# Layer 1's feed-forward by expert tiles: rows scattered to 23 single-expert tiles, gathered weights, results gathered back

## The reference

```python
# layer 1, xn = layernorm(x), 2048 rows of 128
probs = softmax(xn @ gate_w.T)                  # 8 experts
top_idx, top_val = argmax(probs), max(probs)
top_val = top_val / (top_val + 1e-8)
onehot = one_hot(top_idx, 8)
xe = einsum('ne,nd->end', onehot, x_flat)       # a row is zero for all experts but its own
he = gelu(einsum('end,edh->enh', xe, expert_w1))    # 128 -> 256
ye = einsum('enh,ehd->end', he, expert_w2)          # 256 -> 128
out = einsum('end,ne->nd', ye, onehot) * top_val[:, None]
f = layernorm(out) * ln_gamma + ln_beta
# attention of layer 1: 16 heads of 8, window of 32 keys to either side
x = x + attn(xn) * silu(f)
```

## Time and profile before

| | |
|---|---|
| median of 3 runs | 1961.46 us (1961.2 to 1962.14) |
| span of the profiled execution | 1957.4 us |
| the profiled execution's own time | one of the three runs above, which of them is not told |
| median of the runs less the span | 4.1 us |
| TensorE, VectorE, ScalarE, POOL busy | 89%, 73%, 59%, 53% |
| mean granted TensorE clock | 0.951 |
| layer 1, first stage | 951.4 to 1095.6 us |
| layer 1, attention | 1095.6 to about 1312 us |

### The profile page before, as it was taken

The page is one execution under the profiler, slowest core; times in us unless marked ns, Lnnn a source line. Parts: engine busy times, 40 slices in busy tenths (PEclk is TensorE's granted clock), DMA queues, the critical chain, the costliest instruction groups (busy, mean ns, idle before and its releaser), DMA issues. The chain is left out here.

```text
span 1957.4 us, 34440 instructions
## 1 busy us (share of the span) xinstructions
PE 1744.6 (89%) x13171; PEld 1433.1 (73%) x13199; DVE 1421.3 (73%) x2911; ACT 1155.9 (59%) x2340; POOL 1040.4 (53%) x998
## 2 busy tenths in 40 slices
PE   6999999999999999899799788874798568999997
PEld 4888888888888888787567577763577445666676
DVE  6888888788888788534578677857767488777772
ACT  4677767676767777555367555552433344666665
POOL 4888999999999999920312134335257530110111
PEclk9999999999999999999889899986799878999999
DMA  3000000001000000000000000002045300000000
GB/s 90 14 1 15 1 15 1 15 1 36 1 1 1 1 1 1 28 1 1 20 11 22 1 2 2 2 23 69 23 109 133 78 12 1 2 2 2 2 2 23
DMA packets 52100, 37.44 MB, mean 19 GB/s; under 512 B 7560, under 2 KB 45864, under 8 KB 51936
## 3 DMA queue, kind: packets, MB, share of 16 engines
q1 hardware_dynamic: 45248, 30.53, 5.3%
q0 software_dynamic: 5632, 4.20, 1.5%
q10 hardware_dynamic: 1056, 0.52, 0.1%
HBM read 29.99 MB, written 5.24 MB: 18 GB/s over the span
## 5 line engine op out<-in xcount | busy, mean ns | idle before, releaser
L753 POOL TENSOR_TENSOR dtl<-dts,dth 128x512 fp32r<-128x512 f32 x256 | 356.5, 1392 | 20.5
L683 DVE TENSOR_REDUCE nm<-PS 128x1 f32<-128x1024 f32 x256 | 311.6, 1217 | 30.5 <-PE PS L203 29.6
L1930 ACT ACTIVATE ET_a<-PS 128x256 f32<-128x256 f32 (+2 forms) x512 | 223.0, 493 | 129.2 <-PE PS L1845 78.6
L751 POOL CAST dth<-dts 128x512 fp32r<-128x512 f32 x256 | 232.6, 909 | 48.6 <-ACT dts L610 47.5
L201 PE MATMUL PS<-xh,yh 128*128 128x512 f32 x512 | 225.5, 440 | 8.1 <-ACT G L603 4.0
L144 PE MATMUL PS<-C,XN 128*128 128x128 f32 x1120 | 176.3, 283 | 38.1 <-DVE XN L196 34.6
L203 PE MATMUL PS<-xh,yl 128*128 128x512 f32 x512 | 204.7, 400 | 0.0
L202 PE MATMUL PS<-xl,yh 128*128 128x512 f32 x512 | 204.4, 399 | 0.0
L1744 POOL TENSOR_SCALAR_AFFINE_SELECT ET_a<-ET_a 128x1024 f32<-128x1024 f32 x32 | 35.0, 1092 | 310.3 <-ACT ET_a L1930 310.3
L603 ACT ACTIVATE XNT<-PS,nm 128x1024 f32<-128x1024 f32 x128 | 142.8, 1115 | 68.5 <-DVE nm L683 67.3
L610 ACT ACTIVATE dts<-PS 128x512 f32<-128x512 f32 x256 | 152.7, 598 | 45.9 <-POOL dtl L753 43.1
(11 more groups left out here) (425 smaller groups left out, 4709.4 us busy)
## 6 DMA issues: line engine op xcount, KB each, us to landing
e_wg<-in_WgT SPq DMA_DIRECT2D x16, 256.0 KB, 2.8
e_wu<-in_WuT SPq DMA_DIRECT2D x16, 256.0 KB, 3.1
e_wd<-in_WdT SPq DMA_DIRECT2D x16, 256.0 KB, 4.0
X<-in_L_attn_X SPq DMA_DIRECT2D x2, 512.0 KB, 4.5
wqn<-in_L_attn_Wq SPq DMA_DIRECT2D x8, 128.0 KB, 2.1
wkn<-in_L_attn_Wk SPq DMA_DIRECT2D x8, 128.0 KB, 2.6
wvn<-in_L_attn_Wv SPq DMA_DIRECT2D x8, 128.0 KB, 2.4
won<-in_WoT SPq DMA_DIRECT2D x8, 128.0 KB, 2.6
```

The source lines that it names most:

```text
L683: e.tensor_reduce(self.nm[:, half, i:i + 1], self.S[half], AX.X, MAX, negate=True).then_inc(*self.top.up((g, half)))
L751: e.tensor_copy(hi, src).then_inc(*ts.up((g, g4, "h")))
L753: e.tensor_tensor(lo, src, f(hi), SUB).then_inc(*ts.up((g, g4, "l")))
L1930: e.activation(dst, src, ACT.Exp, scale=self.SC, bias=0.0).then_inc(*self.ex.up(it))
```

## The change

`Ffn1` is replaced by `Moe1`. Each row is computed for its own expert alone, in fp32 products without the three-way split.

In the first stage, after the one-hot choice, 18 small bf16 products count for each row how many rows ahead of it have its expert ("ranks"). VectorE makes of it, in 14 steps ("frac" to "row"), each row's place `pos` in a list in which each expert has whole tiles of 128 rows (23 tiles always suffice), and for each tile the row of its expert's weights. POOL zeroes a buffer of 23 tiles, which SP stores to DRAM as `m_x_rows`. The fence to the attention waits for "rk0", the value copies and POOL's last memset. The value copies go from VectorE to ScalarE.

In the attention stage POOL scatters the 16 blocks of rows (`XN`) to `m_x_rows`; SP waits for all 16 and loads the 23 tiles in six transfers; POOL gathers each tile's weights, 128 rows of 2 KB (both matrices), into a ring of 8 slots, a slot being free after the second product of the tile that held it. The jobs of the tiles, T (transpose four tiles), U (first product of two tiles, gelu) and D (second product, copy out), all stand at place (5, 0) of TensorE's and ScalarE's order, and the column products of head 0 wait for the last. SP stores the results, POOL gathers them back to `G` in row order behind the cuts 1 to 6, and multiplies by `top_val` behind the cuts 8 to 11. For this the row products use three banks in heads 0 to 4 and not six; `KH[2]` is cleared by ScalarE after heads 1 and 2; the layernorm steps of `Gate1` run two per head from head 18 on, with `rstd` before cut 17.

```diff
+    def scatter(self, e, q):
+        q.wait_ge(self.blank, "z")
+        q.wait_ge(self.route, "pos")
+        for n in range(NT):
+            e.indirect_dma_start(self.xd[:, :], bass.IndirectOffsetOnAxis(ap=self.pos[:, n:n + 1], axis=0), self.k.XN[:, n, :],
+                                 None).then_inc(*self.sorted.up(n))
+    def weights(self, e, q):
+        q.wait_ge(self.route, "row")
+        for j in range(self.TILES):
+            if j >= self.RING:
+                q.wait_ge(self.on_pe, ("D", (j - self.RING) // 2))
+            e.indirect_dma_start(self.W[:, j % self.RING, :], None, self.k.A["w12"],
+                                 bass.IndirectOffsetOnAxis(ap=self.row[:, j:j + 1], axis=0)).then_inc(*self.in_w[j % self.RING].up(j))
+    def back(self, e, q, x):
+        k = self.k
+        if 1 <= x <= 6:
+            if x == 1:
+                for g in range(6):
+                    q.wait_ge(self.stored[g], "y")
+            for n in range(3 * x - 3, min(3 * x, NT)):
+                e.indirect_dma_start(k.G[:, n, :], None, self.yd[:, :],
+                                     bass.IndirectOffsetOnAxis(ap=self.pos[:, n:n + 1], axis=0)).then_inc(*self.taken.up(n))
...
+        self.place = {}
+        for n_, x in enumerate(self.jobs):
+            self.place.setdefault((5, 0), []).append(x)
...
+    def lift(self, e, q, s):
+        o = self.k.bank(4 + s % 2)
+        q.wait_ge(self.on_act, ("T", s // 2))
+        if s >= 2:
+            q.wait_ge(self.on_act, ("U", s - 2))
+        for j in self.tiles(s):
+            q.wait_ge(self.in_w[j % self.RING], j)
+            for m in range(2):
+                c = 256 * (j % 2) + 128 * m
+                t = e.matmul(o[:, c:c + 128], self.W[:, j % self.RING, 128 * m:128 * m + 128],
+                             self.xT[s // 2 % 2][:, 128 * (j % 4):128 * (j % 4) + 128], start=True, stop=True)
+        t.then_inc(*self.on_pe.up(("U", s)))
...
-        rs, cs, rn, cn = list(range(6)), [], 0, 0
+        rs, cs, rn, cn = list(range(3 if kind == 1 else 6)), [], 0, 0
...
                 if self.kind == 1:
-                    q.wait_ge(self.clear_pool, "edge1")
+                    q.wait_ge(self.clear_edge, 1)
+                    q.wait_ge(self.moe.on_act, self.moe.on_act.last)
...
-            if self.gate and j == 3 and x >= 4 and late < len(self.gate.steps):
+            if self.gate and j in (3, 8) and x >= 18 and late < len(self.gate.steps):
                 self.gate.dve_step(e, q, late)
```

More of the change, by code:

```diff
@@ L1235, in pe, with act @@
                 n = 4 * c + j
-                t = e.matmul(k.bank(4 + c)[:, 128 * j:128 * j + 128], k.XNT[:, 128 * n:128 * n + 128], w.WV, start=True, stop=True)
+                t = e.matmul(k.bank(self.banks[c])[:, 128 * j:128 * j + 128], k.XNT[:, 128 * n:128 * n + 128], w.WV, start=True, stop=True)
             t.then_inc(*self.done.up(c))
+    def act(self, e, q):
+        k, w = self.k, self.w
+        for c in range(4):
+            q.wait_ge(self.done, c)
+            e.activation(w.va[:, 4 * c:4 * c + 4, :, 0:8], k.bank(self.banks[c]).rearrange("p (n h d) -> p n h d", n=4, h=16),
+                         ACT.Copy).then_inc(*self.ready.up(c))
     def dve(self, e, q):
@@ L1368, in pool @@
-    def pool(self, e, q):
[L1369 to L1375, removed]
+        q.wait_ge(self.on_pool, "xs0")
@@ L1432, in act @@
+        e.matmul(flat(self.rank[:, 0:NT, :]), self.bb[:, :], flat(self.oh[:, :, :]), start=True, stop=True)
+        for t0 in range(NT):
+            a = t0 + 1 if t0 else 1
+            n = (NT + 1 if t0 else NT) - a
+            src = bc(self.oh[:, t0, :], [128, 8, n]).rearrange("p e n -> p n e")
+            t = e.matmul(self.rank[:, a:a + n, :], self.ob[:, :], src, start=False, stop=True, skip_group_check=True)
+        t.then_inc(*self.route_pe.up("ranks"))
     def act(self, e, q):
-        k = self.k
@@ new lines, in drop @@
+    def drop(self, e, q, s):
+        q.wait_ge(self.on_act, ("U", s))
+        if s >= 2 and s % 2 == 0:
+            q.wait_ge(self.on_act, ("D", s - 1))
+        for j in self.tiles(s):
+            o = self.k.bank(6)[:, 128 * (j % 4):128 * (j % 4) + 128]
+            for m in range(2):
+                c = 256 * (j % 2) + 128 * m
+                t = e.matmul(o, self.hT[s % 3][:, c:c + 128], self.W[:, j % self.RING, 256 + 128 * m:384 + 128 * m], start=m == 0, stop=m == 1)
+        t.then_inc(*self.on_pe.up(("D", s)))
@@ L1597, in __init__ @@
         self.bank_of, self.before = {}, {}
-        last = {b: first[b] for b in range(4)}
-        rs, cs, rn, cn = list(range(6)), [], 0, 0
+        last = {b: first[b] for b in range(3 if kind == 1 else 4)}
+        rs, cs, rn, cn = list(range(3 if kind == 1 else 6)), [], 0, 0
         rows, cols = [], []
```

366 lines of the change are left out of this document (201 added, 165 removed).

## The result

| | before | changed |
|---|---|---|
| median of the runs, us | 1961.33 (1960.93 to 1962.14, 4 runs) | 1886.95 (1883.49 to 1888.97, 4 runs) |
| ratio | | 0.9616, 95% interval 0.9605 to 0.9628 |
| span of the profiled execution | 1957.4 | 1886.8 (its own time 1888.97) |
| first table load of layer 1 (layer 0's end) | 951.44 | 956.24 |
| from there to the start of layer 2 | 361.60 | 283.40 |

A forecast was written before the change was run, and what follows sets the result against it. TensorE was taken to bound the 104.7 us of expert products, all on the path. Terms -85.3 (first column products), +2.3 (back gathers) and +2.5 (gate steps) gave -80.5, span 1876.9; with 4.1 carried, 1881 us, range 1871 to 1900.

The forecast's parts named there:

- The cut: Layer 1, attention's first memset: waits for the ranks instead of the experts, 1095.75 to 980.0, so -115.8 us.
- so at half clock: The 18 rank products before the attention: TensorE at half clock after an idle, 0.145 us each, 2.6 in all.
- Before the stop: Attention's start to TensorE's stop: 0.5 us for clearing casts on ScalarE, 0.5 for three banks; rows' arrival hidden.
- 1.95: POOL's 16 row scatters: upper bound of their pitch in us, from adding scatters; rows then about 3 us late.
- The lock-out: POOL's 16 scatters give way to VectorE's eight clearing casts: estimated 4 us, inside 6 us of cover, time unchanged.
- The stop: Expert jobs at place (5,0): 29.3 us, bound by POOL's weight gathers, little over TensorE; 0.5 more for a table load.
- Back gathers: POOL's three gathers behind each of cuts 1 to 5 make cuts late: +2.3 us (0 to 12).
- What leaves heads 4 to 17 gains nothing in my sum: Gate steps removed from VectorE in heads 4 to 17: no gain, since TensorE has the tighter budget.
- The doubled steps: Gate's 26 VectorE steps, two per head from head 18: 7.4 us more work over eight heads, priced +2.5 (0 to 5).
- will no longer hide fully: VectorE, 79% busy, gets 18% more work in eight heads from the gate steps: partly exposed, +2.5 us.
- Outside layer 1: Layers 0, 2 and 3: the prediction's sum had no term for them.
- The 4.1 that I carried from span to time: Whole kernel: median 1961.46 lay 4.1 us above the profiled span before; added to span 1876.9 to give 1881.

The follow-up runs named there:

- the three profiles with stalls: Changed kernel with twelve weight slots, 1904.22 us; with gate steps one per head from head 14, 1892.94; with these, POOL's casts first and five jobs in head 4, 1894.09.
- the best kernel of the study: Changed kernel plus twelve slots, gate steps one per head from head 14, POOL's casts first, five jobs in head 4: 1894.09 us, then 1870.49 on another chip.

## Why the prediction was right, and where it was not

Against the profiled span, 1886.8 where 1876.9 was forecast, the terms stand so:

- **The cut**: -118.2, predicted -115.8. The order was right (POOL's last cast late, the routing chain before it). The 18 rank products took 0.8 us and not 2.6, a pitch of 0.044 for those of 8 columns and below the lower bound that I had taken from transposes of 128 columns; "so at half clock" was wrong, the granted clock was 1.00. The steps behind them took 3.7 (3.4).
- **Before the stop**: +0.2, predicted +1.0. The rows were there: TensorE did not wait for them at T(0), and the scatters kept a pitch of 1.26 to 1.56, 1.35 in the mean, so 1.31 was nearly right and 1.95 wrong. The lock-out that was weighed at an estimated 4 us came to 1.3: seven scatters took 1.05 to 1.26 us, each with a VectorE cast of a key buffer running in its first half, the other nine 0.96.
- **The stop**: 30.37 to the first column product, predicted 29.8 with the table load. Gather 8 started 4.9 after T(0), as worked out. A product took 0.223 and not 0.25 (eight records in 1.06), the gathers came 1.25 apart and not 1.31, and against that landings took 4.6 in the median and not 3.0. That POOL's chain and not TensorE bounds it is shown by the two kernels with half rows.
- **Back gathers**: +1.7, as the difference of a kernel with them and one without, both with the steps moved; predicted +2.3.
- **"What leaves heads 4 to 17 gains nothing in my sum, since TensorE, 18.42 of 21 us busy, has the tighter budget"**: wrong, -2.5, with 1.26 and 1.29 in the kernel before. VectorE was part of the pace, though TensorE was the busier engine; through which handover is not shown.
- **The doubled steps**, "**+2.5** (0 to 5)": wrong, +10.7. This is the step that failed. It priced a step by its mean of before, where every one of them stood clear of POOL's cuts, and didn't ask where the cuts fall once there are two per head: a third of them is stretched, to two to four times their length. The eight additional normalisations (7.4) were counted rightly; the 11.6 of stretching were not in the sum. With both VectorE was at 96% from cut 20 to 24, which "will no longer hide fully" understated. That two steps per head cost 10.7 is shown by a run; that the stretching is a good part of it is read from the traces.
- **Outside layer 1**: +4.8 and +2.8 in the profiled execution, at nothing in the sum. Their sum, 7.6, is nearly as large as the 8.2 by which the doubling was missed; single executions of the changed kernel range from 1880.6 to 1889.0, so one profile can't be read closer than that outside the edited stretch. The 4.1 that I carried from span to time is 2.2 in every run of the changed kernel.

So the profiled span came 9.9 above the forecast of it, 2.3 from layer 1 and 7.6 from outside; 1.9 less from span to time, and a median 2.0 under the profiled execution, leave the median 6 above the forecast. In layer 1 the errors are -2.4, -0.8, +0.6, -0.6, -2.5 and +8.2: they add to 2.5, with -0.2 between cut 31 and layer 2 to 2.3, which is the difference of -78.2 and -80.5. The mechanism and the large term were right. That layer 1 came within 2.3 us is luck in part: errors of -6.3 and +8.8 nearly cancel, and with the doubling at its real price and all else as forecast the time would have been 1889.

## What to carry to other kernels

Before work is moved to another place of an engine's program, look at what the neighbour engine does at that place: a duration is worth only as much as the place that it was measured at. Here a VectorE multiply or add of two SBUF tiles that began within one of POOL's cuts of 1.09 us took 1.06 to 1.19 us and not 0.29. And where a ring of buffers feeds a dense stretch, work out when the first slot comes free and how many transfers are left then; idle buffers of other phases can be slots.

## What the runs showed of the hardware that I had not expected

**Stalls without a cause in the program.** The same kernel took 1894.09 us on one chip and 1870.49 on another, while the kernel before took 1958.15 and 1960.41 there. The stalls lie in the stretches of layer 1 where POOL scatters rows, gathers weights and gathers rows back; layers 2 and 3, which have indirect transfers too, took their usual 644 to 645 us. TensorE at the same place of the program, where it stalls (idle time before a row, and its releaser, in brackets):

```profile
993.84 0.59 PE L1923 MATMUL PS<-KH_a,QS_a 128*128 128x256 f32 x2
996.97 0.59 PE L1920 MATMUL PS<-mk,identb 128*128 128x512 bf16 x1 [2.54 <-issue]
...
1005.75 0.80 PE L198 MATMUL PS<-xh,W4h 128*128 128x512 f32 x1 [7.77 <-issue]
```

and where it doesn't:

```profile
994.20 0.59 PE L1923 MATMUL PS<-KH_a,QS_a 128*128 128x256 f32 x2
994.95 0.38 PE L1920 MATMUL PS<-mk,identb 128*128 128x512 bf16 x1 [0.16 <-DVE XNT L2194]
996.26 0.50 PE L198 MATMUL PS<-xh,W4h 128*128 128x512 f32 x1 [0.70 <-DVE QS_a L2110]
```

In the first, VectorE's reduction of that product began 1.8 us after the product's end, and ScalarE waited 9.88 us, for which its row names only a load of half a millisecond before. POOL meanwhile issues its transfers at its usual pace. One more thing sets the three profiles with stalls apart: none of POOL's 119 indirect transfers has a recorded landing in them, where 84 or more have one in the other profiles of kernels with this change. Whether the engines waited for signals or for their instructions, and what differs between the chips, stays open. It matters for measuring: by its time on the first chip alone, the best kernel of the study would have been dropped.

**Indirect transfers.** In the changed kernel a scatter or gather of 128 rows costs POOL mostly 0.94 to 0.96 us (up to 1.26 beside VectorE's casts) and 0.30 to the next, with rows of 512 B or of 2 KB alike; the adding form of the earlier trace rows is dearer. The bytes show in the landing: in the median 2.2 us for a scatter's 64 KB, 3.1 for a gather of half weight rows in sixteen slots, 4.6 for one of 256 KB.
